# Axial attention: packed keys, a head pair on the two row halves of the array, one maximum and one exponential instruction per pair

## The reference, cut to what matters

```python
q = x @ Wq                    # (256, 512) -> 32 heads of 16
k, v = ctx @ Wkv              # (256, 256) @ (256, 1024)
q, k = axial_rope(q, pos), axial_rope(k, pos)     # rotation of pairs, 2 axes
w = softmax(q @ k.T / 4)      # per head, 256 x 256, no mask is in force
x = layernorm(x + (w @ v) @ Wout + bout)
```

## Time and profile before

| | us |
|---|---|
| median of 3 runs (2912.58 to 2915.99) | 2913.66 |
| the profiled execution, its own time | 2908.72 |
| its span, first to last instruction | 2906.9 |
| TensorE busy over the span | 2467.0 (85%) |
| VectorE busy | 1799.7 (62%) |
| ScalarE busy | 1248.9 (43%) |
| GpSimd busy | 297.7 (10%) |

### The profile page before, as it was taken

The page is one execution under the profiler, slowest core; times in us unless marked ns, Lnnn a source line. Parts: engine busy times, 40 slices in busy tenths (PEclk is TensorE's granted clock), DMA queues, the critical chain, the costliest instruction groups (busy, mean ns, idle before and its releaser), DMA issues. The chain is left out here.

```text
span 2906.9 us, 42566 instructions
## 1 busy us (share of the span) xinstructions
PE 2467.0 (85%) x15730; PEld 1904.7 (66%) x15746; DVE 1799.7 (62%) x5199; ACT 1248.9 (43%) x2982; POOL 297.7 (10%) x535
## 2 busy tenths in 40 slices
PE   5889999999974999799999999995888888883674
PEld 4668999998864999476667766763655555551332
DVE  6656767667875666445445544454566666657986
ACT  3434445444433211244344434452544444436663
POOL 3211100001000000000000000002111111101220
PEclk8999999999986999999999999997999999996887
DMA  4101211112005000000000000001000000003001
GB/s 156 62 23 41 70 37 40 69 36 74 29 26 194 1 1 1 1 1 1 1 1 1 1 1 1 1 1 51 5 5 5 5 5 5 5 1 133 1 1 58
DMA packets 41212, 83.41 MB, mean 29 GB/s; under 512 B 4528, under 2 KB 17840, under 8 KB 39856
## 3 DMA queue, kind: packets, MB, share of 16 engines
q1 hardware_dynamic: 41008, 80.70, 7.9%
HBM read 72.30 MB, written 8.39 MB: 28 GB/s over the span
## 5 line engine op out<-in xcount | busy, mean ns | idle before, releaser
L1990 DVE TENSOR_REDUCE s_nmax<-s_a_ps 128x2 f32<-128x512 f32 x256 | 174.3, 686 | 198.7 <-PE s_a_ps L1772 195.7
L651 ACT ACTIVATE s_p<-s_ms,s_nmax 128x256 f32<-128x256 f32 x256 | 128.5, 503 | 192.3 <-DVE s_nmax L754 192.3
L754 DVE CUSTOM_DVE_ANT_0 s_ms<-s_s_ps,s_bias 128x256 f32<-128x256 f32 x256 | 98.2, 421 | 175.9 <-PE s_s_ps L529 175.5
L1375 ACT ACTIVATE l_wo_w<-l_wo_w,s_nmax 128x128 f32<-128x128 f32 (+1 forms) x256 | 114.4, 447 | 197.8 <-DVE s_nmax L1471 197.0
L512 PE MATMUL s_q_ps<-s_xT,s_wh 128*128 128x256 f32 x1024 | 189.6, 286 | 0.0
L1215 PE MATMUL s_s_ps<-l_wqb_w,s_lT 128*128 128x512 f32 x384 | 175.7, 597 | 16.0 <-DVE l_wo_w L1441 15.3
L914 PE MATMUL s_h_ps<-s_xh,s_t 128*128 128x256 f32 x704 | 173.0, 284 | 9.3 <-DVE s_xl L1002 9.3
L1886 ACT ACTIVATE s_pT<-s_s_ps 128x512 f32<-128x512 f32 x256 | 151.6, 606 | 59.6 <-PE s_s_ps L1785 57.3
L562 PE MATMUL s_y_ps<-s_wh,s_oT 128*128 128x512 f32 x512 | 173.0, 399 | 0.0
L914 PE MATMUL s_h_ps<-s_xl,s_t 128*128 128x256 f32 x704 | 172.4, 283 | 0.0
L512 PEld LDWEIGHTS s_q_ps<-s_xT,s_wh 128*128 128x128 f32 x1024 | 165.5, 193 | 6.0 <-issue 0.5
(11 more groups left out here) (304 smaller groups left out, 6686.8 us busy)
## 6 DMA issues: line engine op xcount, KB each, us to landing
s_x_raw<-kept SPq DMA_DIRECT2D x24, 512.0 KB, 3.3
s_c_in<-in_ctx_T SPq DMA_DIRECT2D x32, 256.0 KB, 2.5
l_wqb_w<-in_l_xwq SPq DMA_DIRECT2D x4, 1024.0 KB, 7.8
l_wqb_w<-in_l_xwo SPq DMA_DIRECT2D x4, 1024.0 KB, 10.1
kept<-s_x_raw SPq DMA_DIRECT2D x8, 512.0 KB, 2.7
l_wo_w<-in_l_wo SPq DMA_DIRECT2D x1, 4096.0 KB, 15.5
s_raw<-in_l_w1T SPq DMA_DIRECT2D x2, 2048.0 KB, 9.9
s_raw<-in_l_w2T SPq DMA_DIRECT2D x2, 2048.0 KB, 21.5
```

The lines of the kernel that those rows point to most:

```text
L651: act.activation(p[:, h % PR, q, :], ms[:, h % 2, q, :], ACT.Exp, scale=-1.0, bias=nmax[:, h % PR, q:q + 1], accum_out=den[:, h % PR, q:q ...
L754: dve.tensor_tensor_reduce(ms[:, h % 2, q, :], s_ps[:, h % 2, q * S:(q + 1) * S], bias[:, h // PER % B, :], -SCALE, 3.0e38, ALU.add, ALU.m ...
L1375: act.activation(p[:, h % PR, q, 0:(q + 1) * P], ms[:, h % 2, q, 0:(q + 1) * P], ACT.Exp, scale=-1.0, bias=nmax[:, h % PR, q:q + 1], accum ...
L1990: dve.tensor_reduce(nmax[:, g % 2, :, 2 * pair + e], a_ps[:, n % 2, :].rearrange("p (q k) -> p q k", q=QT), AX_X, ALU.max, negate=True).th ...
```

## The change

- A group's pairs are neighbours now (`head_of`). `kT` holds a pair's keys in one block of 128 rows, without zeros; ScalarE copies it out with one instruction in place of two, and the zeros before the first round go.
- A matmul for the maximum or for the scores runs on 64 rows: head e = 0 on rows 0 to 63 and e = 1 on rows 64 to 127 of the array, the two in turn into different banks. Their number and columns stay. A pair's four matmuls stand together, at even steps only, and fill both banks of `a_ps` or `s_ps`.
- VectorE takes the maxima of a pair with one instruction over 1024 elements; ScalarE its exponentials with one over 1024. Each releases both banks at once.
- `pT` has room for two groups. The outputs of a group are one call of 32 float32 matmuls at every eighth step, in place of two calls of 16.
- The lags and the steps of the projections change: LAG 12, PV_LAG 22, OUT_LAG 23, and the tables in the diff.

```diff
@@ -1560,19 +1560,18 @@
-    LAG = GH + 3
-    QUADS = H // 4
-    QUAD_LAG = LAG + 3 + 2
-    OUT_LAG = QUAD_LAG + 5
-    Q_AT, K_AT, V_AT, Y_AT = (10, 14), (19, 21), (12, 13), (16, 18)
+    LAG = GH + 4
+    PV_LAG = LAG + GH + 2
+    OUT_LAG = PV_LAG + 1
+    Q_AT, K_AT, V_AT, Y_AT = (8, 11), (19, 21), (15, 16), (18, 20)
     XT_AT = (3, 4)
...
     def head_of(n):
-        return n // GH, n % 4, n % GH // 4
+        return n // GH, n % GH // 2, n % 2
     with ExitStack() as ctx:
@@ -1598,11 +1597,11 @@
         qTm = m.sb("qTm", [P, 2, PAIRS, S], F32R)
-        kTz = m.sb("kTz", [P, H, S], F32R)
+        kT = m.sb("kT", [P, H // 2, S], F32R)
         v = m.sb("v", [P, QT, H, 2 * HD])
...
         nmax = m.sb("nmax", [P, 2, QT, GH])
-        pT = m.sb("pT", [P, GH, QT, S])
+        pT = m.sb("pT", [P, 2 * GH, QT, S])
         rden = m.sb("rden", [P, S])
@@ -1767,10 +1766,12 @@
                         pe.wait_ge(t_out, t_turns.at(b - 1, last) + 3)
-                pe.wait_ge(a_out, b * H + n + 1)
+                pe.wait_ge(a_out, b * (H // 2) + n // 2 + 1)
                 for q in range(QT):
-                    mm = pe.matmul(a_ps[:, n % 2, q * S:(q + 1) * S], qTx[:, g % 2, pair, q * P:(q + 1) * P],
-                                   kTz[:, GH * g + 2 * pair + e, :], start=True, stop=True)
+                    for e in range(2):
+                        rows = slice(XD * e, XD * (e + 1))
+                        mm = pe.matmul(a_ps[:, e, q * S:(q + 1) * S], qTx[rows, g % 2, pair, q * P:(q + 1) * P],
+                                       kT[rows, PAIRS * g + pair, :], start=True, stop=True)
                 mm.then_inc(a_full, 1)
@@ -1780,48 +1781,47 @@
                     pe.wait_ge(t_out, t_turns.at(b, (whose if g == G - 1 else "here", "m", g, QT - 1)) + 3)
-                pe.wait_ge(s_out, (b + shift[whose]) * H + n + 1)
+                pe.wait_ge(s_out, (b + shift[whose]) * (H // 2) + n // 2 + 1)
                 for k in range(QT):
-                    mm = pe.matmul(s_ps[:, n % 2, k * S:(k + 1) * S], kTz[:, GH * g + 2 * pair + e, k * P:(k + 1) * P],
-                                   qTm[:, g % 2, pair, :], start=True, stop=True)
+                    for e in range(2):
+                        rows = slice(XD * e, XD * (e + 1))
+                        mm = pe.matmul(s_ps[:, e, k * S:(k + 1) * S], kT[rows, PAIRS * g + pair, k * P:(k + 1) * P],
+                                       qTm[rows, g % 2, pair, :], start=True, stop=True)
                 mm.then_inc(s_full, 1)
-            def outputs(b, m):
-                g, e = m // 2, m % 2
-                pe.wait_ge(s_out, b * H + 2 + 4 * m + 4)
-                if e == 0:
-                    pe.wait_ge(o_out, b * G + g + 1)
-                for k in range(QT):
-                    for part in range(2):
-                        for pair in range(PAIRS):
-                            ones_or_values = one[:, e, :] if part else v[:, k, GH * g + 2 * pair + e, :]
-                            mm = pe.matmul(o_ps[32 * pair:32 * pair + 32, part, :], ones_or_values,
-                                           pT[:, 4 * e + pair, k, :], start=(e == 0 and k == 0 and part == 0),
-                                           stop=(e == 1 and k == QT - 1 and part == 1))
+            def outputs(b, g):
+                pe.wait_ge(s_out, b * (H // 2) + 1 + PAIRS * (g + 1))
+                pe.wait_ge(o_out, b * G + g + 1)
+                for e in range(2):
+                    for k in range(QT):
+                        for part in range(2):
+                            for pair in range(PAIRS):
+                                ones_or_values = one[:, e, :] if part else v[:, k, GH * g + 2 * pair + e, :]
+                                mm = pe.matmul(o_ps[32 * pair:32 * pair + 32, part, :], ones_or_values,
+                                               pT[:, GH * (g % 2) + 2 * pair + e, k, :],
+                                               start=(e == 0 and k == 0 and part == 0),
+                                               stop=(e == 1 and k == QT - 1 and part == 1))
                 mm.then_inc(pv_done, 1)
...
                 for n in range(H):
-                    if has(b, "here"):
+                    if n % 2 == 0 and has(b, "here"):
                         greatest(b, n)
...
                     whose = "prev" if n < LAG else "here"
-                    if has(b, whose):
+                    if n % 2 == 0 and has(b, whose):
                         scores(b, whose, (n - LAG) % H)
-                    whose = "prev" if n < QUAD_LAG else "here"
-                    if n % 4 == QUAD_LAG % 4 and has(b, whose):
-                        if whose == "here" and n == QUAD_LAG:
+                    whose = "prev" if n < PV_LAG else "here"
+                    if n % GH == PV_LAG % GH and has(b, whose):
+                        if whose == "here" and n == PV_LAG:
                             pe.wait_ge(f_out, f_turns.at(b, ("here", "v", QT - 1)) + 2)
-                        outputs(b + shift[whose], (n - QUAD_LAG) % H // 4)
+                        outputs(b + shift[whose], (n - PV_LAG) % H // GH)
                     for use in f_turns.steps[n]:
@@ -1833,7 +1833,7 @@
                 project(0, n, "qk"[n // QT], n % QT, x_at=1)
-            pe.wait_ge(fixed, 4)
+            pe.wait_ge(fixed, 2)
             for n in range(2 * QT):
@@ -1845,16 +1845,13 @@
             act.sem_inc(t_out, 2)
-            act.sem_inc(s_out, 2)
+            act.sem_inc(s_out, 1)
             act.sem_inc(xs_free, 1)
...
                            ACT.Sin).then_inc(sines, 1)
-            act.wait_ge(fixed, 1)
-            act.copy(kTz[0:XD, 1::2, :], blank[0:XD, :].unsqueeze(1).broadcast_to([XD, H // 2, S])).then_inc(fixed, 1)
             def rows_over(at, bank, of, g, q):
@@ -1868,10 +1865,7 @@
                 elif of == "k":
-                    heads = slice(GH * g, GH * (g + 1), 2)
-                    act.copy(kTz[0:XD, heads, cols], t[0:XD])
-                    heads = slice(GH * g + 1, GH * (g + 1), 2)
-                    act.copy(kTz[XD:P, heads, cols], t[XD:P]).then_inc(t_out, 1)
+                    act.copy(kT[:, PAIRS * g:PAIRS * (g + 1), cols], t).then_inc(t_out, 1)
                 else:
@@ -1879,11 +1873,12 @@
             def exponentials(b, j):
-                if j % 4 == 0:
-                    act.wait_ge(pv_done, b * QUADS + j // 4 + 1)
-                act.wait_ge(s_full, b * H + j + 1)
-                act.activation(pT[:, j % GH, :, :], s_ps[:, j % 2, :].rearrange("p (k n) -> p k n", k=QT),
+                if j % GH == 0:
+                    act.wait_ge(pv_done, b * G + j // GH + 1)
+                act.wait_ge(s_full, b * (H // 2) + j // 2 + 1)
+                two = slice(j % (2 * GH), j % (2 * GH) + 2)
+                act.activation(pT[:, two, :, :], s_ps[:, :, :].rearrange("p e (k n) -> p e k n", k=QT),
                                ACT.Exp).then_inc(s_out, 1)
@@ -1892,12 +1887,12 @@
                     whose = "prev" if n < LAG else "here"
-                    if has(b, whose):
+                    if n % 2 == 0 and has(b, whose):
                         exponentials(b + shift[whose], (n - LAG) % H)
...
                 rows_over(q, q % 2, "x", 0, q)
-            act.wait_ge(fixed, 4)
+            act.wait_ge(fixed, 2)
             for n in range(2 * QT):
@@ -1909,7 +1904,7 @@
             dve.sem_inc(f_out, 1)
-            dve.sem_inc(a_out, 2)
+            dve.sem_inc(a_out, 1)
             dve.sem_inc(o_out, 1)
@@ -1932,10 +1927,6 @@
             dve.wait_ge(sines, 1)
-            dve.wait_ge(fixed, 1)
-            dve.tensor_copy(kTz[XD:P, 0::2, :], blank[XD:P, :].unsqueeze(1).broadcast_to([XD, H // 2, S])).then_inc(fixed, 1)
             for t in range(2):
@@ -1966,7 +1957,7 @@
                 if q == 0:
-                    dve.wait_ge(pv_done, b * QUADS + 2)
+                    dve.wait_ge(pv_done, b * G + 2)
                 t = f_ps[:, :].rearrange("p (h d) -> p h d", h=H)
@@ -1986,11 +1977,12 @@
                 g, pair, e = head_of(n)
-                dve.wait_ge(a_full, b * H + n + 1)
-                dve.tensor_reduce(nmax[:, g % 2, :, 2 * pair + e], a_ps[:, n % 2, :].rearrange("p (q k) -> p q k", q=QT),
+                dve.wait_ge(a_full, b * (H // 2) + n // 2 + 1)
+                dve.tensor_reduce(nmax[:, g % 2, :, 2 * pair:2 * pair + 2].rearrange("p q e -> p e q"),
+                                  a_ps[:, :, :].rearrange("p e (q k) -> p e q k", q=QT),
                                   AX_X, ALU.max, negate=True).then_inc(a_out, 1)
-                if n % GH == GH - 1:
-                    dve.wait_ge(a_out, b * H + 2 + n + 1)
+                if n % GH == GH - 2:
+                    dve.wait_ge(a_out, b * (H // 2) + 1 + n // 2 + 1)
                     high, low = qx[:, g, :, :, 3 * HD], qx[:, g, :, :, 3 * HD + 1]
@@ -1999,7 +1991,7 @@
             def sums_of_outputs(b, g):
```

(4 more changed lines are left out.)

## The result

| | before | after |
|---|---|---|
| median of four runs on one chip, us | 2913.99 (2912.58 to 2915.99) | 2955.47 (2951.67 to 2958.48) |
| profiled execution, its own time | 2908.72 | 2953.19 |
| its span | 2906.9 | 2951.4 |
| the stage | 639.5 | 682.0 |

The ratio after to before is 1.0141, 95% interval 1.0124 to 1.0159: slower by 41 us. The prediction was 2896, faster, with a range up to 2938. It was wrong in sign, and the time lies outside its range.

What follows compares the result with a forecast made beforehand. TensorE sets the pace, but not alone. Crediting 2.4 us a round, less 1 for the tail, gives about 18 off: 2908.7 - 18 = 2891, plus 5 for the median, 2896 us; own range 2880 to 2912, whole range 2862 to 2938.

Steps and rivals of the forecast that it cites:

- The switch, 0.2 us per block: TensorE entering and leaving a block of 64 rows: 0.2 us, 28 blocks a round, 5.6 us; bounds nothing and 0.3.
- The credited 72.3: Forecast length of a round in us, crediting only 2.4 us of gain against 74.7 before.
- the layout: The prediction's quarter-by-quarter schedule of the round after: sum 71.4 us against 74.7, 3.3 less.
- The clock, taken as 1.00 throughout: TensorE's granted clock; a fall towards 0.5 in longer last-quarter waits was named only as what would make the forecast wrong.
- rival (2): The two halves do not run together, a pair still costs 0.48 us and switches are paid: 2934 us, chance 0.25.
- 0.43 us for these four loads: TensorE's weight loads of a pair, were the two halves to queue; 1.6 of the 7.7 us gain would be left.
- The durations of maximum and exponential: VectorE's maximum over 1024 elements at 1.22 us, ScalarE's exponential over 1024 at about 1.03 us.
- the wait of the first quarter: TensorE waiting in steps 0 to 7 for VectorE's reciprocal and reduction: 2 us, in a quarter of 12.4 us.
- second and third quarter: Steps 8 to 23, with TensorE's eight projections: together 43.2 us where they took 44.6.
- The fourth: The quarter of steps 24 to 31, bounded by VectorE: end at 15.8 us, before 16.6.
- Rival (3): Halves run together, but the banks' single turn and VectorE's queue swallow 2.1 of the 2.4 us: 2911 us, chance 0.13.
- The tail: After the rounds, the last group's outputs wait for all its exponentials: gives 1 us back.

Runs made afterwards that it cites:

- full-row kernel: The changed kernel with every maximum and score matmul over all 128 rows of the packed keys, so no halves and no switches: 2948.15 us, 1.0126.
- Filler: The changed kernel with 8 extra float32 matmuls per round, results not used, placed where TensorE waits for the maxima: 2932.55 us, 1.0072.
- halves alone: The kernel before with packed keys and each head's matmuls on its 64 rows, one head per step, nothing side by side: 2969.61 us, 1.0202.
- joined kernel: The changed kernel with a step's transposes behind its scores (16 blocks on halves, not 28) and the row norm at step 30: 2943.69 us, 1.0100.
- kernel in which VectorE empties first: The joined kernel with norm at step 30, VectorE taking `f_ps` ahead of the maximum at steps 16 and 20, no filler: 2909.08 us, 0.9984.

## Why the prediction was wrong

**Two steps failed; one makes the change worth nothing, the other makes it slower.**

1. *The switch, 0.2 us per block.* It was sized from changes to and from the column strips. In the prediction's own terms a block and the transposes behind it take 0.24 + 0.2 + 0.37 = 0.81 us; measured are 0.44 + 0.46 = 0.90 (2324.40 to 2325.30). So the switch is 0.29, just under the upper bound of 0.3, and more than the 0.24 that a pair saves in a block. For 28 blocks that is at most 2.5 us of TensorE more per round; by the six tenths of a round in which the forecast held TensorE to be the bound, 1.5 on the path. The credited 72.3 becomes 73.8, and with the clock held up the round measured 75.1. Most of the 1.3 left is read from rows of the kernel after: TensorE waits 0.34 us for a bank of `t_ps` in the first quarter (2327.54), which the layout does not have, and from a y projection to the key projection behind its sum it is 4.58 and 4.49 us where the layout has 4.05. The full-row kernel shows the switch from the other side: without halves and without switches the time is not worse.

```profile
2358.97 3.70 PE L1752 MATMUL s_f_ps<-s_wo,s_oT 128*128 128x512 f32 x8
...
2363.55 1.95 PE L1752 MATMUL s_f_ps<-s_wk,s_cT 128*128 128x512 f32 x4 [0.58 <-DVE s_r L1973]
```

2. *The clock, taken as 1.00 throughout.* It stood in the prediction's last lines as what would make it wrong, with no price in the sum, no rival and no chance. It should have had all three: the layout itself had TensorE wait 2 us and more in the first and fourth quarter, and the stage's first projection had shown matmuls at half speed behind 9.72 us of idling. In the trace after the fourth quarter falls to 0.66, round 0 and the last part to 0.84. Filler takes back 20 to 23 us of the 41; for the rest the clock is a reading, since the stretches that no filler reached are the ones that stayed long (62.4 us at 0.86 in round 0, against 57.6 at 0.97 before).

That the clock costs this much is shown. What brings it down is shown in part. The prediction named TensorE's longer waits. Filler in the waits lifts the clock, so they take part; but the kernel before keeps 1.00 with 5.2 us of waits in its fourth quarter, and the halves alone, with shorter waits, run at 0.90 to 0.92. So matmuls on 64 rows are a cause beside the waits, which neither the prediction nor the two theories had. No run tells what it is about them: the rows, the two running at a time, or the time lost in the switches.

**What held.** The halves run together (four loads in 0.30 us as two before):

```profile
2324.40 0.30 PEld L1773 LDWEIGHTS s_a_ps<-s_kT,s_qTx 64*128 64x128 f32 x4 [1.98 <-DVE s_nmax L1981]
```

So rival (2) had the right side by a mechanism that is false, and its price per pair, 0.48, was about 0.25 in truth. The prediction's estimate from the Trainium skill (TensorE: Matmul & The Clock Gate, LDWEIGHTS), 0.43 us for these four loads if those of the two halves queued, is not borne out: they do not queue. The durations of maximum and exponential, the wait of the first quarter (put at 2 us, 1.84) and its 12.4 us (measured 13.0) held; second and third quarter were put at 43.2 and took 45.6, by the switch and the longer way behind the y projections. The fourth was put at 15.8 and took 16.5 with the clock held up. Rival (3) has two halves. The single turn of the banks swallows nothing: releasing them singly left the time as it was. VectorE's queue in the middle quarters does cost: TensorE waits 1.75 and 1.81 us there for `f_ps` behind a reduction, and with the order changed in two steps the joined kernel is 35 us faster. The layout had these two waits and counted them, so they are not where the sum went wrong, but they were the better place to look for a gain.

**The tail.** The prediction gave it 1 us. With no round behind it TensorE waits 1.1 to 1.5 us at a time for the exponentials of a whole pair, and the group's outputs begin only behind the last of them:

```profile
2632.13 0.50 PE L1788 MATMUL s_s_ps<-s_qTm,s_kT 64*128 64x256 f32 x4 [1.48 <-ACT s_pT L1881]
...
2642.70 0.64 PE L1803 MATMUL s_o_ps<-s_pT,s_v 128*32 128x256 f32 x8 [1.12 <-ACT s_pT L1881]
```

From the last full round to the stage's end it is 21.5 us more. In the first filler kernel that part took 169.8 and not 182.2, so 12 of them go with the clock; how the other 9 divide between these waits and the clock of the drain was not told apart.

**Left open.** Why rounds of one kernel differ in clock (0.93 and 1.00 above) with nothing else changed. What holds the clock of the kernel in which VectorE empties first at 0.87, where TensorE's waits for maxima are down to 5.6 us a round. And which property of the 64-row matmuls brings the clock down; the packed kernel with maxima and scores on 128 rows and filler, or the kernel before with filler and halves, would tell more.

## What to carry to other kernels

Before work is taken from the engine that sets the pace, look whether the engine behind it is near: where TensorE then waits for VectorE several times in a row, its clock can fall and take back more than was saved, the more so, by the runs here, where its matmuls run on half the rows. Give the clock a term and a chance of its own in the sum. Price a change of tile shape per block and count the blocks; group them before anything else. Remove the waits by the order in the queue of the other engine first, then fill what is left, and test a saving with filler in place to see what it is worth by itself.

## What the runs showed of the hardware

- Four matmuls of 64 rows and 256 columns in fp32r on both halves cost as much as two on one half (0.44 and 0.43 us between transposes).
- A block on 64 rows between transposes costs 0.19 us on entering and 0.17 on the transposes behind it, of which 0.3 is the change of rows (a head's matmuls behind transposes cost 0.06 or 0.07 more before, too).
- The granted clock fell to 0.50, the 1.2 GHz level, for 13 us: it fell behind a wait of 1.8 us, and waits of 1.3 and 2.9 followed. In the round before the change waits of 1.1, 1.35, 1.6, 0.65 and 1.6 us left it at 1.00. The Trainium skill (TensorE: Matmul & The Clock Gate, HAM oscillation) puts such falls down to a long idle gap; here short ones were enough.
- With matmuls on 64 rows the clock fell in a wait of 0.94 us; with the packed kernel's matmuls on all 128 rows it held, in the round shown, through waits of 1.5 and 1.3 us and fell in one of 3.55.
- VectorE's instructions on 128x2 take 0.16 to 0.94 us in the fourth quarter, while GpSimd is busy for 10.4 of 19.9 us; in the joined kernel with the norm at 30 the one that took 0.94 takes 0.17. The Trainium skill (GPSIMD Engine Reference, Specifications) names contention for SBUF between the two engines, for VectorE's instructions with two inputs in SBUF or in a mode that uses two ports; that it is the cause here was not tested.
